# The first stage of a two-layer conv and token-mixing kernel, rebuilt: fewer taps on POOL, one statistics round for two norms, sums taken along with the products

## What is computed

```
x = x + depthwise3x3(ln_c(x), conv_kernel)        # ln_c: norm over the 64 channels, eps 1e-6
t = tokens of x
Wx = ln_t(t) @ W.T                                # ln_t: norm over the 64 channels, eps 1e-5
Wx = (Wx - mean) * rsqrt(var + 1e-5) * gamma + beta   # mean, var per channel over all tokens and batches
y_t = sigmoid(Wx_t + y_(t-1) @ V.T)               # a scan over the positions
t = t + y
```

## Time and profile before

| | us |
|---|---|
| median of the runs | 1888.73 |
| the profiled execution | 1891.77 |
| its span, first to last instruction | 1890.0 |
| first stage (stage block) | 19.7 to 757.4 |
| channel statistics | 758.9 to 765.8 |
| scan | from 766.0 |
| busy PE, POOL, DVE, ACT over the span | 1537.0, 1478.3, 1415.1, 1236.0 |
| mean granted TensorE clock | 0.907 |

### The profile page before, as it was taken

The page is one execution under the profiler, slowest core; times in us unless marked ns, Lnnn a source line. Parts: engine busy times, 40 slices in busy tenths (PEclk is TensorE's granted clock), DMA queues, the critical chain, the costliest instruction groups (busy, mean ns, idle before and its releaser), DMA issues. The chain is left out here.

```text
span 1890.0 us, 24219 instructions
## 1 busy us (share of the span) xinstructions
PE 1537.0 (81%) x5627; PEld 635.5 (34%) x5627; DVE 1415.1 (75%) x2290; ACT 1236.0 (65%) x2177; POOL 1478.3 (78%) x1092
## 2 busy tenths in 40 slices
PE   3899999999999995499992769999999999825200
PEld 1333333333333331266651423333333333204200
DVE  1779999999998986499994547999999999961000
ACT  2777777777777762399992458889888898620000
POOL 2999999999999994048889129999999999911475
PEclk8999999999999997699997789999999999965555
DMA  4578888888878755859996527898888887652011
GB/s 153 165 219 250 251 254 239 249 245 250 254 235 257 229 173 177 334 216 421 424 405 269 214 48 220 282 293 287 284 272 282 289 290 245 205 163 48 1 2 2
DMA packets 111405, 429.80 MB, mean 227 GB/s; under 512 B 44672, under 2 KB 47648, under 8 KB 66208
## 3 DMA queue, kind: packets, MB, share of 16 engines
q1 hardware_dynamic: 91376, 423.77, 68.6%
q10 hardware_dynamic: 16432, 4.29, 1.4%
q0 software_dynamic: 3456, 0.19, 0.2%
HBM read 257.89 MB, written 170.01 MB: 226 GB/s over the span
## 5 line engine op out<-in xcount | busy, mean ns | idle before, releaser
L445 ACT ACTIVATE tap_products<-xn,kk 128x512 f32<-128x512 f32 x384 | 275.1, 718 | 165.7 <-POOL x_and_products L476 160.3
L476 POOL TENSOR_TENSOR x_and_products<-tap_products,x_and_products 128x512 f32<-128x512 f32 x256 | 327.0, 1277 | 41.7 <-POOL x_and_products L476 3.6
L376 PE MATMUL pst<-xn,taps 128*128 128x512 f32 x768 | 351.4, 593 | 0.0
L1462 POOL TENSOR_SCALAR exp_q<-exp_q 128x512 f32<-128x512 f32 x128 | 189.6, 1482 | 74.2 <-ACT exp_q L1413 74.2
L534 DVE SCALAR_TENSOR_TENSOR pst<-xn,kk,pst 128x512 f32<-128x512 f32 x256 | 192.1, 750 | 62.2 <-PE pst L376 62.0
L879 DVE SCALAR_TENSOR_TENSOR pss<-region,bn,pss 128x256 f32<-128x256 f32 x432 | 195.7, 489 | 45.8 <-PE pss L791 44.6
L376 PEld LDWEIGHTS pst<-xn,taps 128*128 128x128 f32 x768 | 145.4, 190 | 186.1 <-issue 186.1
L1457 POOL TENSOR_TENSOR sq_norm<-x_ring 128x512 f32<-128x512 f32 x128 | 188.6, 1473 | 5.4 <-DVE x_ring L1509 1.7
L476 POOL TENSOR_TENSOR x_and_products<-tap_products,x_ring 128x512 f32<-128x512 f32 x128 | 164.4, 1285 | 19.8 <-ACT tap_products L445 19.7
L828 POOL TENSOR_TENSOR x_block<-x_block,region 128x2048 f32<-128x2048 f32 x28 | 155.6, 5556 | 18.5 <-DMA x_block<-x_scratch 13.5
L416 ACT ACTIVATE sq<-x_ring 128x512 f32<-128x512 f32 x256 | 157.7, 622 | 16.2 <-POOL x_ring L483 10.1
(11 more groups left out here) (239 smaller groups left out, 2947.0 us busy)
## 6 DMA issues: line engine op xcount, KB each, us to landing
rstd_wide<-rstd_scratch SPq DMA_DIRECT2D x128, 512.0 KB, 7.1
x_ring<-in_x SPq DMA_DIRECT2D x32, 1024.0 KB, 5.3
x_scratch<-x_ring SPq DMA_DIRECT2D x32, 1024.0 KB, 4.3
xl_scratch<-wx SPq DMA_DIRECT2D x32, 1024.0 KB, 8.6
region<-xl_scratch SPq DMA_DIRECT2D x32, 1024.0 KB, 12.3
x_ring<-x_scratch SPq DMA_DIRECT2D x32, 1024.0 KB, 5.5
rstd_of_channels<-rstd_scratch SPq DMA_DIRECT2D x64, 512.0 KB, 7.6
out<-x_ring SPq DMA_DIRECT2D x32, 1024.0 KB, 6.6
```

The costliest lines, as they stand in the source:

```text
L376: m = pe.matmul(wide(pst[g % 2]), taps[:, n * P:(n + 1) * P], tap_rows(g, t), start=(n == 0), stop=(n == len(PE_TAPS) - 1))
L445: act.activation(prod[:, n, :, :], tap_rows(g, t), ACT.Copy, scale=kk[:, t:t + 1]).then_inc(products, 1)
L476: pool.tensor_tensor(xr[:, g % XR, :], prod[:, n, :, :].rearrange("p r w -> p (r w)"), xr[:, g % XR, :] if n else x_tile(g), ALU.add).then ...
L1462: pool.tensor_scalar(e, e, 1.0, None, ALU.min).then_inc(clipped, 1)
```

## The change

- Taps go by pairs of tiles: PE takes 2 in every tile (taps 3, 4), DVE 4 in an even and 5 in an odd tile, ACT and POOL 3 and 2. Per four tiles: PE 8 for 12, DVE 18 for 12, ACT with POOL 10 for 12. The ring of three products goes on over the tiles.
- One statistics round serves both norms: norm 1 of block k and norm 2 of block k-4. The mean matrices are 32 wide with 16 live columns for each norm and add up in one PSUM bank; 36 rounds in place of 64, so one mean square, variance, Ln and Exp for two norms. The eps is per partition, from the constants. The clamp moves from DVE to ACT, as a Relu. SP writes and broadcasts the rows of both norms in one go, norm 1 first.
- PE writes the W product and norm 2's statistics to PSUM in step order (inner dimension of the output 32 elements apart), so that `scale_wx` reads contiguous operands and writes runs of 32.
- `scale_wx` also gives its sum per channel; `square_u` on ACT, two steps later, squares the result with a sum. `bn_stats` goes. The short block reduces the sums, needs one matmul, and takes the variance as mean square less squared mean.
- Lags: `square` of x1 12, `project` 20, `scale_wx` 21, norm 2's rounds 16; `load` seven steps ahead instead of eight.
- The `reached` buffer of the scan gets its own memory, where it used that of the statistics.

```diff
             XSLOTS = 8
             RT = 8
             XR = 3
-            NP, ND = len(ACT_TAPS), len(DVE_TAPS)
+            NP = 3
+
+            def taps_of(g):
+
+                return ((PE_TAPS[:2], [5, 6, 7, 8], [0, 1, 2]),
+                        (PE_TAPS[:2], [2, 5, 6, 7, 8], [0, 1]))[g % 2]
+
+            dve_taps, act_taps = ([sum(len(taps_of(i)[who]) for i in range(g)) for g in range(NT + 1)] for who in (1, 2))
...
-            SQ, CENTER, TAPS, SUMS, FINISH, SQ1, PROJECT, SCALE = -4, 5, 8, 9, 10, 10, 18, 19
-            STATS = (0, 14)
+            SQ, CENTER, TAPS, SUMS, FINISH, SQ1, PROJECT, SCALE = -4, 5, 8, 9, 10, 12, 20, 21
+            STATS = (0, 16)
+            BEHIND = (STATS[1] - STATS[0]) // TPB
+            ROUNDS = NBLK + BEHIND
             STEPS_A = NT + SCALE + 6
 
-            order = sorted((TPB * k + STATS[l], l, k) for l in range(2) for k in range(NBLK))
-            round_of = {(l, k): n for n, (_, l, k) in enumerate(order)}
+            def round_of(l, k):
+                return k + BEHIND * l
+
+            def norms_in(n):
+
+                return [(l, n - BEHIND * l) for l in range(2) if 0 <= n - BEHIND * l < NBLK]
+
+            def rstd_written(n):
+
+                return rstd_out[n % 2], sum(16 * B * len(norms_in(m)) for m in range(n % 2, n + 1, 2))
 
...
+
+            def by_step(row):
+
+                return row.rearrange("p (n c) -> p c n", n=CLEN)
+
+            def in_chunks(row):
+                return row.rearrange("p (c n) -> p c n", n=CLEN)
+
+            def stepped(row):
+                return row.rearrange("p (n c) -> p n c", n=CLEN)
+
+            def u_steps(g):
+
+                c0 = g % TPB * (TILE // CLEN)
...
-                def rstd_to_dram(l, k):
-                    n = round_of[l, k]
+                def rstd_to_dram(n):
                     sp.wait_ge(rstd_ready, n + 1)
-                    for b in range(B):
-                        sp.dma_start(rstd_d[l][k, b, :].rearrange("(j n) -> j n", n=TILE),
-                                     rstd[16 * b:P:32, n % 2, :]).then_inc(rstd_out[n % 2], 16)
+                    for l, k in norms_in(n):
+                        for b in range(B):
+                            sp.dma_start(rstd_d[l][k, b, :].rearrange("(j n) -> j n", n=TILE),
+                                         rstd[16 * l + 8 * b:P:32, n % 2, :]).then_inc(rstd_out[n % 2], 16)
 
                 def rstd_to_channels(l, k):
-                    n = round_of[l, k]
-                    sp.wait_ge(rstd_out[n % 2], 32 * (n // 2 + 1))
+                    if l == 0 or k >= NBLK - BEHIND:
+                        sp.wait_ge(*rstd_written(round_of(l, k)))
...
-                    if (k := block_at(t, -8)) is not None:
+                    if (k := block_at(t, -7)) is not None:
...
-                    else:
-                        pe.wait_ge(x1_ready, TPB * (k + 1))
+                def by_norm(l, row):
+
+                    return by_step(row) if l else in_chunks(row)
+
+                def stats_of(n):
+
+                    norms = norms_in(n)
+                    for l, k in norms:
+                        if l == 0:
+                            pe.wait_ge(*loaded_x(k))
+                        else:
+                            pe.wait_ge(x1_ready, TPB * (k + 1))
                     if n:
                         pe.wait_ge(msq_done, n)
-                    for j in range(TPB):
-                        m = pe.matmul(psm[32 * j:32 * j + 32, :], stat32[:, :], x_tile(TPB * k + j), start=True, stop=True)
+                    for l, k in norms:
+                        for j in range(TPB):
+                            x_in = in_chunks(x_tile(TPB * k + j))
+                            m = pe.matmul(by_norm(l, psm[32 * j:32 * j + 32, :]), stat_of[:, l, :], x_in,
+                                          start=(l, k) == norms[0], stop=(l, k) == norms[-1])
                     m.then_inc(mean_ready, 1)
-                    pe.wait_ge(squared[l], TPB * (k + 1))
+                    for l, k in norms:
+                        pe.wait_ge(squared[l], TPB * (k + 1))
                     if n:
                         pe.wait_ge(clamped, n)
-                    for j in range(TPB):
-                        m = pe.matmul(pse[32 * j:32 * j + 32, :], stat32[:, :], sq[l][:, j, :], start=True, stop=True)
+                    for l, k in norms:
+                        for j in range(TPB):
+                            x_in = in_chunks(sq[l][:, j, :])
+                            m = pe.matmul(by_norm(l, pse[32 * j:32 * j + 32, :]), stat_of[:, l, :], x_in,
+                                          start=(l, k) == norms[0], stop=(l, k) == norms[-1])
                     m.then_inc(second_ready, 1)
...
                     if g >= 2:
-                        pe.wait_ge(acc_step, ND * (g - 1))
-                    for n, t in enumerate(PE_TAPS):
+                        pe.wait_ge(acc_step, dve_taps[g - 1])
+                    mine = taps_of(g)[0]
+                    for n, t in enumerate(mine):
                         m = pe.matmul(wide(pst[g % 2]), taps[:, n * P:(n + 1) * P], tap_rows(g, t),
-                                      start=(n == 0), stop=(n == len(PE_TAPS) - 1))
+                                      start=(n == 0), stop=(n == len(mine) - 1))
...
-                    pe.matmul(psw[g % 2][:, :], wcT[:, :], x_tile(g), start=True, stop=True).then_inc(wx_ready, 1)
+                    pe.matmul(by_step(psw[g % 2][:, :]), wcT[:, :], in_chunks(x_tile(g)), start=True,
+                              stop=True).then_inc(wx_ready, 1)
...
-                    n = round_of[l, k]
+                def rsqrt(n):
+                    act.wait_ge(var_done, n + 1)
+                    if n:
+                        act.wait_ge(ln_done, n)
+                    act.activation(var[:, :], pse[:, :], ACT.Relu).then_inc(clamped, 1)
                     act.wait_ge(clamped, n + 1)
                     if n:
                         act.wait_ge(rstd_ready, n)
-                    act.activation(ln[:, :], var[:, :], ACT.Ln, bias=(eps_c, eps_t)[l]).then_inc(ln_done, 1)
+                    act.activation(ln[:, :], var[:, :], ACT.Ln, bias=eps_rows).then_inc(ln_done, 1)
                     act.wait_ge(ln_done, n + 1)
                     if n >= 2:
-                        act.wait_ge(rstd_out[n % 2], 32 * (n // 2))
+                        act.wait_ge(*rstd_written(n - 2))
                     act.activation(rstd[:, n % 2, :], ln[:, :], ACT.Exp, scale=-0.5).then_inc(rstd_ready, 1)
+
+                def square_u(g):
+                    act.wait_ge(u_ready, g + 1)
+                    if g:
+                        act.wait_ge(u_squared, g)
+                    act.activation(u_squares[:, :].rearrange("p (n c) -> p n c", n=CLEN), u_steps(g), ACT.Square,
+                                   accum_out=sums[:, 1, g:g + 1]).then_inc(u_squared, 1)
 
                 def tap_product(g, n):
...
-                    if g >= 1:
-                        act.wait_ge(product_added, NP * (g - 1) + n + 1)
-                    t = ACT_TAPS[n]
-                    act.activation(prod[:, n, :, :], tap_rows(g, t), ACT.Copy,
+                    q, t = act_taps[g] + n, taps_of(g)[2][n]
+                    if q >= NP:
+                        act.wait_ge(product_added, q - NP + 1)
+                    act.activation(prod[:, q % NP, :, :], tap_rows(g, t), ACT.Copy,
                                    scale=kk[:, t:t + 1]).then_inc(products, 1)
...
-                    if n == ND - 1:
+                    if n == len(taps_of(g)[1]) - 1:
                         if g >= 2:
                             dve.wait_ge(x1_ready, g - 1)
                         out = acc[:, g % 2, :, :]
-                    t = DVE_TAPS[n]
+                    t = taps_of(g)[1][n]
                     dve.scalar_tensor_tensor(out=out, in0=tap_rows(g, t), scalar=kk[:, t:t + 1], in1=wide(pst[g % 2]),
...
-                        dve.wait_ge(bn_done, TPB * (k - 1))
-                    c0 = g % TPB * (TILE // CLEN)
-                    by_chunk = u[:, k % 2, :].rearrange("p (n c) -> p c n", n=CLEN)[:, c0:c0 + TILE // CLEN, :]
-                    dve.tensor_tensor(by_chunk, psw[g % 2][:, :].rearrange("p (c n) -> p c n", n=CLEN),
-                                      rb[1][:, k % 2, cols_of(g % TPB)].rearrange("p (c n) -> p c n", n=CLEN),
-                                      ALU.mult).then_inc(u_ready, 1)
-
-                def statistics(g):
-                    dve.wait_ge(u_ready, TPB * (g // TPB + 1))
...
+                    dve.scalar_tensor_tensor(out=u_steps(g), in0=stepped(psw[g % 2][:, :]), scalar=1.0,
+                                             in1=stepped(rb[1][:, k % 2, cols_of(g % TPB)]), op0=ALU.mult, op1=ALU.mult,
+                                             accum_out=sums[:, 0, g:g + 1]).then_inc(u_ready, 1)
 
                 for t in range(0, STEPS_A):
```

(28 more changed lines are left out.)

110 lines of the change are left out of this document (51 added, 59 removed).

## The result

The changed kernel takes 1866.91 us (median of 4 runs, 1865.05 to 1868.19), the kernel before beside it on the same chip 1889.53 us (4 runs, 1888.72 to 1892.98). The ratio is 0.9874, 95% interval 0.9858 to 0.9889: faster by 22 us or 1.3%, where 53 us were forecast. The profiled execution took 1866.96 us, with a span of 1865.2 us and a mean granted clock of 0.904.

A forecast was written before the change was run, and what follows sets the result against it. The prediction took POOL's four operations (5.30 us per tile) as the bound, falling to 4.95 set by DVE and the round trip: 8.4 + 40 + 4.4 = 53 us gained, to 1836 us, range 1808 to 1886.

The forecast's parts named there:

- the early tiles: First 12 tiles, without scaling or second norm: POOL decides, 5.30 to 4.60 us per tile, 8.4 us gained.
- the middle: The other 115 tile intervals: period from 5.30 to 4.95 us, 0.35 each, 40 us gained.
- the ends: Setup and end of the stage: 2.0 and 3.6 us gained, 0.45 and 0.8 lost, together 4.4 us gained.
- rival C: Round trip longer than counted (transfers meeting, SP late): period 5.05 to 5.25 us, 1848 to 1872 us; chance 0.19.
- What bounds the kernel before: POOL runs its four operations per tile with hardly a wait and sets the 5.30 us period.
- POOL after, 4.60: POOL with 10 additions instead of 12 in four tiles: 18.4 us, 4.60 per tile.
- rival B: Strided PSUM output makes PE's passes dearer; at twice the pass 5.7 us per tile, 1922 us; chance 0.15.
- the heavy step: PE's step with merged statistics, centre, taps and W product: 7.1 us in a 4.9 step, 0.6 to 0.9 spare.
- DVE, 4.84: DVE's work after the change: 19.4 us in four tiles, 4.84 per tile, with the scaling at 0.75 us.
- The round trip: Variance, rows to DRAM, broadcasts, scaling four steps later: 16.7 to 17.7 us, so period at least 4.71 to 4.96.
- Rival D: DVE cheaper than counted, so POOL's 4.60 us per tile is reached: 93 us gained, 1796 us; chance 0.06.
- Rival E: Operations leave POOL but the period stays at 5.3 to 5.45 us: 1876 to 1894 us; chance 0.06.

The follow-up runs named there:

- Run 9: Run 1's kernel with the old tap shares (three each for PE, DVE, and ACT with POOL; POOL four operations a tile): 1887.39 us.
- run 6: Changed kernel with second norm's broadcast ahead of the first's, and variance ahead of the scaling in steps without a tap: 1806.36 us.
- run 4: Changed kernel, but PE writes the W product contiguously in PSUM and DVE's scaling reads it in steps of 16 elements: 1865.79 us.
- run 7: Run 6's kernel with one more tap moved from DVE to PE in each fourth tile: 1823.09 us.
- Run 1: Changed kernel, but SP issues the second norm's broadcast ahead of the first norm's, same transfers and bytes: 1812.27 us.
- run 3: Changed kernel, but DVE takes the variance ahead of the scaling in steps without a tap: 1859.84 us.
- run 8: Run 1's kernel with W product contiguous in PSUM and the scaling in old chunk order, writing u in steps of 512 bytes: 1861.91 us.

## Why the prediction was right in direction and wrong in size

Forecast were 8.4 us for the early tiles, 40 for the middle and 4.4 for the ends; measured are 7.2, 17.8 and -0.2 (the ends with the rest). So 22 of the 28 missing us lie in the middle, and 4.6 in the ends. The measured time lies in the range of rival C (1848 to 1872), which had a chance of 0.19, and C's mechanism is what the runs show.

- **What bounds the kernel before: right.** POOL's four operations. Run 9 puts them back and gets the old time. It gives PE its third tap back too, but POOL waits 0.0 us ahead of `finish` there, so it is POOL that has no time left, and not PE that is late.
- **POOL after, 4.60: right** (4.59 in run 6; in the changed kernel the first 12 intervals, 57.0 us less one wait of 1.8 for DVE, give 4.60).
- **PE's strided output at nothing: right, rival B is refuted.** 591 against 592 ns a pass (run 4), and the merged round lasts 432.94 - 429.37 = 3.57 us (forecast 3.7). The sentence of the Trainium skill (PSUM — Partial Sum Buffer, Specifications (TRN2)) on non-contiguous patterns does not hold for these fp32 passes: the measurement decides. That the heavy step is thin but not on the path held for the change; run 7 shows how thin.
- **DVE, 4.84: the term was 0.16 too high.** It is 4.68. The scaling starts its successor 0.61 us after itself (431.76 to 432.37), as the low end had it, not 0.75: 0.14 for every tile, as the accumulator read of 81 ns lies inside the scaling's tail. Dependent taps are 0.785 to 0.79 apart (420.05 to 420.84), as taken.
- **The round trip: the step that failed, in size.** The place was named, four steps and nothing late between them, and the rival C for it; the trip was counted too short, and with it the period. Forecast: 14.7 to 15.7 us from the first write to the scaling; measured 16.8. (The 4.4 us in it from the first write to the end of the store are 4.1 by the rows, 415.88 to 420.) By its terms: broadcasts issued 3.33 us after the first write (forecast from the earlier trace rows, 2 x 1.07 and the store's issue: right), their data from about 428 to 437.9, that is 5.8 us after the first write and 9.9 long, where 5.5 and 8.8 to 9.8 were taken (both edges are my reading of the windows); and from the end of the data to the scaling 1.1 us instead of 0.4. The runs don't show why this last part is longer. The forecast's argument that a late chain shortens its own start did not come true: the first write is issued 2.08 us after the end of the variance, and 1.98 had been counted. From the end of the variance (420.14) to the scaling there are 18.9 us, against 16.7 to 17.7, and 2.0 more to the end of the next variance, so the block takes 20.8 us here and 20.6 on average, against 19.8. Those 0.8 us in 115/4 blocks are 22 us: the whole gap between 40 forecast and 17.8 measured for the middle. Run 1 takes the first norm's broadcast out of this trip, changes nothing else, and the period falls to DVE's own 4.68. In the forecast I had also taken 4.95 as a point between two limits that meet in one instruction (4.84 and 4.96); of two such limits the higher one alone counts, so its upper end should have been the middle of the range.
- **POOL's wait and DVE's wait, as signs:** POOL idle ahead of `finish` on `acc` was forecast at 0.3 us a tile and is 66.5/128 = 0.52; DVE's wait for `rstd_wide` below 1 us per block and is 1.9.
- **ACT: counted at 4.1, measured 3.72** (472.26/127), and not on the path either way.
- **The first 12 tiles: right**, 7.2 for 8.4. **First `finish`:** forecast 1.25 later for copies and a fourth tap, measured 1.2 earlier. The setup is 0.43 later (DVE's first normalisation at 41.69 for 41.26), as forecast; but DVE's waits for PE behind it are 1.10 and 0.86 shorter (3.94 to 2.84 ahead of the fourth normalisation, 1.88 to 1.02 ahead of the first tap), and the variance's clamp of 0.60 is gone from between the taps. I had counted only what was added. As the first `finish` of kernels with this same setup lies anywhere from 53.6 to 55.6, one trace doesn't tell that the change gained 1.2 here, and neither that it lost 1.25.
- **The end: one term right, one wrong, one missed.** Statistics block 3.7 (forecast 3.6). `bn_stats` behind the last scaling: forecast 2.0, measured 0, since it had lain beside the landing of the last store. Missed: the merged round's variance behind the late scaling, -5.7; run 3 gives back 3.4 of it in the trace. What the other 2.3 are is not shown.
- **Rival D (1796)** needed the trip to be short enough, which runs 1 and 6 brought. Even then DVE's 4.68 and not POOL's 4.60 decides. **Rival E** is refuted by the period, 5.144 where E had 5.3 or more.

The sum again with measured terms: 1.2 + 7.2 + 17.8 - 5.7 + 3.7 + 0.6 = 24.8 us of span.

## What to carry to other kernels

When two rounds of small transfers are merged, work out the whole trip for the consumer that has least time, and put that consumer's transfer first in the queue: the swap of two broadcasts was worth 55 us where the change itself had brought 22. An engine freed of work pays only until the next limit, so before tuning further, change the order of what is queued; and ask of every transfer that is moved what idle gap it had filled. Look at the last round by itself, since an order that is harmless while the pipeline runs can hold up its end.

## What the runs showed of the hardware

- DVE's fp32 tensor operation of 128x512 takes 684 ns when it writes SBUF in runs of 32 elements, and when it writes in steps of 512 bytes 1081 ns (kernel before) or 1115 ns (run 8, where one source is stepped too). A page of the Trainium skill (Vector Engine (DVE) Microarchitecture Reference, 5.2 Measured stream behaviour on trn2) has 1.054 ns a column for contiguous operands and 1.71 for a destination that hops 4 KiB with each element, a ratio of 1.62. The traces are close to it, with 1081/684 = 1.58 and 1115/684 = 1.63, for a smaller hop.
- Steps in PSUM cost nothing: PE's pass writes it in steps of 32 elements in 591 ns (592 contiguous), and DVE reads it in steps of 16 elements in 685 ns (684 contiguous).
- A broadcast of one row to 64 partitions moves 220 GB/s with the DMA engines full (1.03), the store ahead of it 365 and the transfers behind it 430. A queue of four transfers is thus not priced by its bytes alone.
- DMA at 0.94 of its time and 278 GB/s (run 1, 100 us in the middle) still didn't bound the stage: DVE was busy for 98.29 of these 100 us.
- A wait put down to "issue" was one for a DMA: in the drain of the same kernel the wait ahead of the same instruction has the releaser `rstd_wide` (9.88 us), and run 1, which only moves that transfer ahead of its neighbour, takes all of it away.
